# In the odd steps of an attention block on one core: the block of the mix multiplied ahead of the pair of maxima

## The reference, cut to what matters

```python
mod = (silu(c) @ wmod).reshape(16, 6, 1, 256)             # sa, ca, ga, sb, cb, gb per batch
h = layernorm(x) * (1 + ca) + sa                          # x: 16 x 1024 x 256
q = (h @ Wq.T) in 8 heads of 64;  kv = h @ Wkv_down.T     # kv: 64 wide, shared by all heads
k, v = kv @ Wk_up.T, kv @ Wv_up.T                         # 8 heads of 64
attn = softmax(q k^T * 64**-0.5);  x = x + ga * (attn v) @ Wo.T
h = layernorm(x) * (1 + cb) + sb
x = x + gb * (h @ weight.T + pooled(h) @ disha)
```

## Time and profile before

| | us |
|---|---|
| median of 3 runs | 3064.16 |
| lowest and highest | 3061.7 and 3064.53 |
| the profiled execution, its own time | 3062.38 |
| its span | 3060.3 |
| mean granted TensorE clock | 0.997 |

### The profile page before, as it was taken

The page is one execution under the profiler, slowest core; times in us unless marked ns, Lnnn a source line. Parts: engine busy times, 40 slices in busy tenths (PEclk is TensorE's granted clock), DMA queues, the critical chain, the costliest instruction groups (busy, mean ns, idle before and its releaser), DMA issues.

```text
span 3060.3 us, 45405 instructions
## 1 busy us (share of the span) xinstructions
PE 3009.4 (98%) x15394; PEld 1695.4 (55%) x15394; DVE 2143.6 (70%) x2548; ACT 1719.3 (56%) x3210; POOL 2546.1 (83%) x1520
## 2 busy tenths in 40 slices
PE   6999999999999999999999999999999999999998
PEld 4445555555555555555555555555555555555545
DVE  5566767767677676766767677676776767667665
ACT  3556555555555555555565555555555555555544
POOL 3788887888888888888888879888888888888787
PEclk9999999999999999999999999999999999999999
DMA  3111121121112111111211211211121111111111
GB/s 85 43 49 43 53 67 46 53 63 46 53 50 67 46 53 54 52 60 46 60 46 53 67 46 51 64 48 53 50 65 48 50 57 51 60 39 53 46 49 46
DMA packets 166166, 162.94 MB, mean 53 GB/s; under 512 B 62256, under 2 KB 114096, under 8 KB 165936
## 3 DMA queue, kind: packets, MB, share of 16 engines
q1 hardware_dynamic: 165936, 160.05, 17.9%
HBM read 74.40 MB, written 17.33 MB: 30 GB/s over the span
## 4 chain that ended last, share of the span: by engine, by line
PE 95%; DVE 2%; POOL 1%; ACT 1%; DMA 1%; issue 0%; SPq 0%; DVEq 0%; ACTq 0%; POOLq 0%
PE ps_mix L653 29%; PE ps_score L674 18%; PE ps_score L676 15%; PE ps_max L702 11%; PE ps_side L639 7%; PE ps_side L768 5%; PE ps_side L787 3%; PE ps_side L754 2%; POOL prob_sum L1050 1%; PE ps_side L775 1%; PE ps_side L720 1%; PE ps_side L744 1%; DVE neg_max L1202 1%; ACT probs L879 1%; PE ps_side L735 0%
## 5 line engine op out<-in xcount | busy, mean ns | idle before, releaser
L1050 POOL TENSOR_TENSOR prob_sum<-prob_sum,probs 128x1024 f32<-128x1024 f32 x768 | 1862.5, 2425 | 347.3 <-ACT probs L879 271.6
L1202 DVE TENSOR_REDUCE neg_max<-ps_max 128x1 f32<-128x1024 f32 x1024 | 1204.2, 1217 | 303.3 <-PE ps_max L702 299.3
L879 ACT ACTIVATE probs<-ps_score 128x512 f32<-128x512 f32 x2048 | 1112.3, 597 | 477.1 <-PE ps_score L676 457.4
L653 PE MATMUL ps_mix<-probs,values 128*64 128x512 f32 x4096 | 935.4, 598 | 0.8 <-ACT probs L879 0.8
L674 PE MATMUL ps_score<-query,key_hi 128*128 128x512 f32 x2048 | 880.0, 430 | 9.8 <-ACT probs L879 6.4
L676 PE MATMUL ps_score<-query_m,key_lo 128*128 128x512 f32 x2048 | 808.6, 395 | 0.0
L653 PEld LDWEIGHTS ps_mix<-probs,values 128*64 128x64 f32 x4096 | 271.3, 136 | 532.7 <-issue 531.5
L674 PEld LDWEIGHTS ps_score<-query,key_hi 128*128 128x128 f32 x2048 | 384.2, 188 | 258.0 <-ACT probs L879 96.6
L676 PEld LDWEIGHTS ps_score<-query_m,key_lo 128*128 128x128 f32 x2048 | 386.2, 189 | 45.4
L702 PE MATMUL ps_max<-key_hi,query 64*128 64x512 f32 x2048 | 376.1, 445 | 9.6 <-DVE neg_max L1202 7.1
L1050 POOL TENSOR_TENSOR prob_sum<-probs 128x1024 f32<-128x1024 f32 x128 | 311.8, 2436 | 58.3 <-ACT probs L879 58.2
(11 more groups left out here) (199 smaller groups left out, 2864.1 us busy)
## 6 DMA issues: line engine op xcount, KB each, us to landing
query_m<-query SPq DMA_DIRECT2D x128, 256.0 KB, 2.4
query_m<-query SPq DMA_DIRECT2D x256, 128.0 KB, 2.6
recip<-recip_scratch SPq DMA_DIRECT2D x254, 128.0 KB, 2.9
x_in<-in_L_attn_x_dram SPq DMA_DIRECT2D x32, 512.0 KB, 4.7
x_mid<-in_L_attn_x_dram SPq DMA_DIRECT2D x64, 256.0 KB, 3.1
out_dram<-x_mid SPq DMA_DIRECT2D x64, 256.0 KB, 2.2
denoms<-recip SPq DMA_DIRECT2D x508, 1.0 KB, 1.7
gates<-gates_scratch SPq DMA_DIRECT2D x16, 256.0 KB, 4.5
```

What stands on the lines that cost most here:

```text
L653: last = nc.tensor.matmul(ps_mix[j * R:j * R + R, :], values[par][:, k, :], probs[:, (STEPS * z.c + s) % RING, j * HALF:(j + 1) * HALF], s ...
L879: nc.scalar.activation(probs[:, (STEPS * z.c + s) % RING, half * HALF:(half + 1) * HALF], ps_score[half], ACT.Exp, scale=SCALE).then_inc(e ...
L1050: nc.gpsimd.tensor_tensor(out=total[:, :], in0=before, in1=probs[:, now % RING, :], op=ALU.add).then_inc(adds_done, 1)
L1202: nc.vector.tensor_reduce(neg_max[:, col:col + 1], ps_max[j][:, :], AX_X, ALU.max, negate=True).then_inc(maxima_done, 1)
```

## The change

In the steps that have both a pair of maxima and a block of the mix (s % 4 = 1), TensorE multiplies the block of the mix first and the pair of maxima after it. Nothing else is touched: the same instructions with the same operands and semaphores, and the streams of the other engines as they were.

```diff
--- before.py
+++ after.py
@@ -839,8 +839,8 @@
             def slot(z):
                 for s in range(STEPS):
                     scores(z, s)
+                    mixes(z, s)
                     maximum(z, s)
-                    mixes(z, s)
                     side_work(z, s)
 
             run_slots(pe, slot)
```

## The result

The changed kernel takes 3095.35 us (median of 4 runs, 3093.93 to 3097.23), the kernel before 3062.93 us beside it on the same chip (3061.14 to 3064.53): a ratio of 1.0105, 95% interval 1.0093 to 1.0117. So it is slower by 1.05%, 32 us; 3089 us was forecast. The span of the profiled execution is 3092.6 us against 3060.3.

What follows compares the result with a forecast made beforehand. TensorE, busy 98% without gaps in the middle, was taken to bound the kernel. Four late side pieces sum to 23.5 us, with small ones 25: profiled 3062.4 becomes 3087.4, plus 1.8 for the median, 3089 us; range 3070 to 3108.

Steps and rivals of the forecast that it cites:

- the cover over VectorE's step: TensorE's block of the mix, 3.58 us, during which VectorE takes each pair of maxima; the change moves it.
- Nothing is added or left out ... I cost this at 0: TensorE's matmuls: four changes of kind before and after, cost 0, bound -25 to +25 us over 252 blocks.
- The four places: Steps 53, 61, 5 and 13: multiply held by an addition, later side piece late by 0.61, 0.64, 0.20, 0.20 us.
- One sign of being right: VectorE's multiplies of steps 5, 13, 53 and 61 were to take 2 us or more.
- The faster rival: Mix weights load while the scores run, 0.10 us in 252 blocks: 3039 us without waits, 3064 with; 7%.
- the one without waits: Multiplies miss GpSimd's additions, the waits don't come, nothing is late: no change, 3064 us; 15%.
- the reading of the port as bandwidth that is shared evenly: VectorE's multiply beside an addition takes twice its 0.69 us at most; step 53 in time, sum near 0.
- some small ones: Small losses that couldn't be placed, which took the sum from 23.5 to 25 us.
- in 21, 29 and 37 the reductions end late in an addition or between two, so that the multiply is short: VectorE in steps 21, 29 and 37: these come out with room, no loss forecast.
- Splits in steps 23, 31, 39, 43 and 47 stand behind reductions that aren't moved: VectorE's splits in these steps: taken as not delayed by the change, no loss forecast.
- The third rival: Multiplies of 29 and 37 blocked too, delays pile up: 1 to 2 us per batch more, 3105 to 3115 us; 13%.
- The maxima after those get 3.58 us more room: TensorE's maxima following those of s % 4 = 3, which need the earlier reductions, get 3.58 us more room.

Runs made afterwards that it cites:

- the run with 17 and 21: Only steps 17 and 21 have the mix ahead of the maxima, against the kernel before: 3069.65 us, ratio 1.0019.

## Why the prediction was right, and where it wasn't

**The sign and the mechanism were right.** TensorE had no wait to give back, the blocks cost the same in the new order, and the cover over VectorE's step was what the change moved. "Nothing is added or left out ... I cost this at 0" held: the new order costs nothing with the multiply one step later (0.9999), and in the changed kernel the mix and the maxima keep their 3.58 and 0.66 us. **The four places held**, each in every batch or all but one, and that the addition is the reason was shown by moving it. One sign of being right was off: the multiply of step 61 takes 1.81 us in most batches, not 2 or more, since the two statistics ahead of it take up part of the addition's time; it ends no earlier for that. The faster rival and the one without waits are out, and the reading of the port as bandwidth that is shared evenly too: 2.44 us, not 1.4.

**Mis-sized terms.** The four places were forecast at 0.61, 0.64, 0.20 and 0.20 us and measured 0.53, 0.52, 0.15 and 0.14. In step 53, 0.07 us of it is that VectorE begins its next operation ahead of the recorded end of the one before (1540.81 against 1538.44 + 2.44), which the sum added up end to start. Over the 14 batches they make 18.2 us of the 30.7, where the forecast's terms make 23.1 (14 x 1.65). The 1.5 us that the forecast added for "some small ones" came from no row.

**The steps that failed.** That "in 21, 29 and 37 the reductions end late in an addition or between two, so that the multiply is short" was read with GpSimd where it stood before. In step 21 the multiply takes 1.82 us, because GpSimd is late by then. And "Splits in steps 23, 31, 39, 43 and 47 stand behind reductions that aren't moved" is wrong for 23: its reductions start 1.72 us after their maxima (1446.90 - 1445.18), where it was 0.84 in the kernel before (1430.03 - 1429.19). These two make the loss of step 25, 0.66 us per batch or 9 us in all; the single losses of steps 24, 40 and 47 add 3.4 us. Both were put at nothing, while the four named places came out 5 us too dear. So it is partly luck that 25 us forecast and 32 measured lie this near: two misses of opposite sign. The third rival, delays that pile up, was right that a multiply blocked from its start delays what stands behind it, but placed the chain at steps 29 and 37 of every batch. It came there once: in step 37 of batch 4 the multiply takes 2.84 us and the query piece of step 40 waits 1.23.

"The maxima after those get 3.58 us more room" was put down as a remark. The run with only s % 8 = 5 swapped shows that it carries the result: without it multiplies as long as these cost 87 us in place of 32.

## What to carry to other kernels

When a long block on the busiest engine moves past another one, write down for each engine behind it which work the block covered and which work it covers afterwards; both change, and a half-made move can be the worst of all. An operation on a shared port has no fixed length: price it by what the other engine has begun at that moment, in both directions, and don't assume that the other engine stays where it stood. Before giving up such a move, look whether the covered engine's own order can follow it; here one step more of delay for one multiply gave all of the loss back.

## What the hardware showed that I had not expected

- The port works both ways. A multiply that finds an addition running takes 2.44 us in place of 0.69, and an addition that finds a split running is recorded with 3.28 us in place of 2.40. The second kind is a delay that GpSimd carries along for eight steps. In the run with 17 and 21, 0.1 us of order decides over 2 us of a short split's length: 0.41 us where it began 0.15 us ahead of an addition, 2.58 where the addition began 0.08 us ahead of it.
- Where a run of matmuls with 128x128 weights and 512 columns meets another kind, about 0.10 us is lost on either side: the last takes 0.32 us to the start of a mix or of maxima, the first behind them 0.34 to the next, for 0.23 inside the run. One more break costs 0.2 us per block. Between the mix and the maxima no price shows: 3.58 and 0.66 us in either order.
- The recorded waits of TensorE understate the loss: 0.28 us recorded, 0.53 us lost.
- From 95 to 105 us, behind the waits of the start-up, four of the fourteen profiled executions run at 1.2 GHz (granted clock 0.50 to 0.52). It costs about 5 us (an estimate, half of those 10), some 0.16% of the time. One and the same kernel can differ by that much: the four executions with all but step 21 swapped took 3082.3 and 3083.6 us at a mean granted clock of 0.997, 3088.7 at 0.995, and 3092.9, the profiled one, at 0.994.
